# An unread TensorE product ahead of each entry of maxima in the first three steps of a group

## The reference

```
def _L0_attn_ref(x, wq, wk, wv, wo):
    DIM = 512
    N_HEADS = 32
    N_KV_HEADS = 8
...
    hd = D // H
    q = (x @ wq).reshape(B, N, H, hd)
    k = (x @ wk).reshape(B, N, J, hd)
    v = (x @ wv).reshape(B, N, J, hd)
    q = _rope(q, ROPE_THETA)
    k = _rope(k, ROPE_THETA)
...
    scores = jnp.einsum('bhqd,bhkd->bhqk', q, k) / jnp.sqrt(jnp.float32(hd))
    causal = jnp.tril(jnp.ones((N, N), dtype=bool))
    scores = jnp.where(causal[None, None], scores, -jnp.inf)
    weight = jax.nn.softmax(scores, axis=-1)
    out = jnp.einsum('bhqk,bhkd->bhqd', weight, v)
    out = out.transpose(0, 2, 1, 3).reshape(B, N, D)
    return out @ wo
...
    x = L0_attn_x
    xn = _layernorm(x, axis=-1)
    x = x + _L0_attn_ref(xn, L0_attn_wq, L0_attn_wk, L0_attn_wv, L0_attn_wo) + _L0_ffn_ref(xn, L0_ffn_W_up, L0_ffn_W_gate, L0_ffn_W_down)
    xn = _layernorm(x, axis=-1)
    x = x + _L1_attn_ref(xn, L1_attn_Wq, L1_attn_bq, L1_attn_Wk, L1_attn_bk, L1_attn_Wv, L1_attn_bv, L1_attn_Wg, L1_attn_bg) + _L1_ffn_ref(xn, L1_ffn_Wa, L1_ffn_Wp, L1_ffn_w_std, L1_ffn_w_rec)
    return x
```

## Time and profile before

| | us |
|---|---|
| median of 3 runs | 2506.42 |
| the runs | 2490.51, 2506.42, 2521.99 |
| the profiled execution, its own time | 2503.88 |
| its span (first to last instruction) | 2502.1 |
| mean granted TensorE clock in it | 0.974 |

### The profile page before, as it was taken

One profiled execution on the slowest core, in us unless ns is written; L12 is line 12 of the kernel. 1 busy time (PEld: TensorE's weight loads), 2 busy tenths in 40 slices (PEclk: granted clock), 3 DMA queues, 4 the chain that ended last, 5 costly groups with the idle time before them and its releaser, 6 DMA issues. The chain is left out here.

```text
span 2502.1 us, 41728 instructions
## 1 busy us (share of the span) xinstructions
PE 2368.4 (95%) x16236; PEld 1472.2 (59%) x16236; DVE 1743.1 (70%) x2135; ACT 1268.4 (51%) x2432; POOL 510.6 (20%) x444
## 2 busy tenths in 40 slices
PE   8989999999999999999999889989999999999988
PEld 5778877764444444444444557778865555455545
DVE  6664556557888888888683353432279999999986
ACT  4522222227777777877676432222225666556653
POOL 2210000010000000000000002220036766667752
PEclk9999999999999999999799989999999999999999
DMA  6771100014112121120003220007861232220024
GB/s 226 239 190 55 41 27 1 1 21 71 29 36 35 23 54 26 32 41 19 8 22 78 70 85 1 1 0 149 251 143 33 51 70 68 69 52 24 13 80 145
DMA packets 119507, 161.47 MB, mean 65 GB/s; under 512 B 60624, under 2 KB 66288, under 8 KB 113934
## 3 DMA queue, kind: packets, MB, share of 16 engines
q1 hardware_dynamic: 114058, 142.91, 23.1%
q10 hardware_dynamic: 5124, 15.73, 2.0%
q0 software_dynamic: 128, 0.16, 0.0%
HBM read 110.90 MB, written 47.69 MB: 63 GB/s over the span
## 5 line engine op out<-in xcount | busy, mean ns | idle before, releaser
L929 ACT ACTIVATE a_ex<-a_ps_s 128x512 f32<-128x512 f32 (+3 forms) x1280 | 621.4, 533 | 218.4 <-PE a_ps_s L995 141.8
L1085 DVE TENSOR_REDUCE first_space<-a_ps 128x2 f32<-128x1024 f32 (+2 forms) x532 | 541.7, 1047 | 107.6 <-PE a_ps L960 104.7
L1426 ACT ACTIVATE a_ex<-a_ps_s 128x512 f32<-128x512 f32 (+3 forms) x640 | 320.5, 532 | 260.1 <-PE a_ps_s L1520 138.8
L1393 POOL TENSOR_TENSOR a_acc<-a_acc,a_ex 128x512 f32<-128x512 f32 (+3 forms) x288 | 348.9, 1212 | 116.5 <-ACT a_ex L1426 97.9
L1040 PE MATMUL a_ps_o<-a_ex,a_v 128*32 128x256 f32 (+2 forms) x5016 | 359.0, 368 | 8.2 <-ACT a_o L917 7.3
L1596 DVE TENSOR_REDUCE a_mx_part<-a_ps 128x2 f32<-128x1024 f32 (+2 forms) x320 | 336.6, 1055 | 26.3 <-PE a_ps L1472 23.0
L2094 POOL TENSOR_TENSOR gc_z<-gc_state,gc_qg 128x512 f32<-128x512 f32 x16 | 26.3, 1642 | 1078.7 <-DVE gc_qg L2082 1078.7
L1629 DVE TENSOR_TENSOR a_acc<-a_acc,a_ex 128x512 f32<-128x512 f32 (+3 forms) x288 | 243.0, 844 | 2.7 <-ACT a_ex L1426 2.4
L995 PE MATMUL a_ps_s<-a_q,a_k 50*128 50x512 f32 (+2 forms) x720 | 239.9, 414 | 1.9 <-ACT a_ex L929 1.9
L960 PE MATMUL a_ps<-a_k,a_q 48*128 48x512 f32 (+2 forms) x720 | 218.1, 406 | 2.9 <-DVE first_space L1085 2.3
L1040 PEld LDWEIGHTS a_ps_o<-a_ex,a_v 128*32 128x32 f32 x5016 | 104.9, 109 | 166.5 <-ACT a_ex L929 105.6
(11 more groups left out here) (289 smaller groups left out, 4597.2 us busy)
## 6 DMA issues: line engine op xcount, KB each, us to landing
a_q<-q SPq DMA_DIRECT2D x30, 256.0 KB, 4.8
a_k<-k SPq DMA_DIRECT2D x15, 512.0 KB, 4.8
a_q<-q SPq DMA_DIRECT2D x15, 512.0 KB, 6.2
q<-first_k SPq DMA_DIRECT2D x22, 256.0 KB
first_q<-q SPq DMA_DIRECT2D x18, 256.0 KB, 5.1
second_q<-q SPq DMA_DIRECT2D x9, 512.0 KB, 5.5
second_k<-k SPq DMA_DIRECT2D x9, 512.0 KB, 4.6
X<-in_x SPq DMA_DIRECT2D x4, 1024.0 KB, 13.8
```

The source lines that it names most:

```text
L929: act.activation(ex[unit % NE][:, h % 2, off:CH], ps_s[n % 3][:, off:CH], ACT.Exp, scale=SCALE)\
L1085: dve.tensor_reduce(mx_part[:, 2 * p:2 * p + 2, i, kc], bank[:, :, 0:w], AX.X, ALU.max).then_inc(taken1, 1)
L1393: pool.tensor_tensor(total[:, off:CH], total[:, off:CH], tile, ALU.add).then_inc(added0, 1)
L1426: act.activation(ex[s % NE][:, h, off:CH], ps_s[n % 3][:, off:CH], ACT.Exp, scale=SCALE)\
```

## The change

In steps (0,0), (0,1) and (0,2) of every group, each entry of maxima gets one unread product of 512 columns ahead of it. The first six steps of the attention keep their two. `s < FINAL + STEPS` holds for all steps.

```
--- before.py
+++ after.py
@@ -723,6 +723,7 @@
     STEP_LIST = [(g, c, t) for g in range(GROUPS) for c, t in PASS2_STEPS]
     FINAL = len(STEP_LIST) - STEPS
     FILLED = 6
+    SEAM = ((0, 0), (0, 1), (0, 2))
     TAIL = FINAL + 23
     UNIT_AT = {TAIL + 2 * u: u for u in range(2 * KT)}
     SLOTS = {s: range((s + LEAD) * PAIRS, (s + LEAD + 1) * PAIRS) for s in range(len(STEP_LIST))}
@@ -1056,7 +1057,7 @@
                     if n in FLIP_AT:
                         flip(n)
                     if n < len(BLOCKS):
-                        max_scores(n, 2 if s < FILLED else 0)
+                        max_scores(n, 2 if s < FILLED else 1 if (c, t) in SEAM and s < FINAL + STEPS else 0)
                     if p == 1 and (s in UNIT_AT or s - 1 in UNIT_AT):
                         first = s in UNIT_AT
                         if s == TAIL:
```

## The result

The changed kernel takes 2514.46 us in the median of 20 runs (2509.3 to 2556.7); the kernel before, in 20 runs beside it, 2504.88 (2485.83 to 2535.75). The ratio is 1.0069 with a 95% interval from 1.0039 to 1.0099: 0.7% slower, which is no change by a measure of 2%, but a loss beyond its own interval. The profiled execution took 2512.05 us.

What follows compares the result with a forecast made beforehand. The late seam was bound by VectorE, the early seam and rest of the group by TensorE's order; 2503.88 - 15.1 (clock fall removed) + 18.0 (42 products) = 2506.8, predicted as 2507 us, range 2492 to 2524.

Steps and rivals of the forecast that it cites:

- The mechanism: Products fill TensorE's thin stretch in the seam, so the clock stays up; they cost about as much as the fall prevented.
- the signs named: Groups 1 to 7 2.57 us longer (wrong under 1.0 or over 3.5), 66 fill matmuls, no stretch at 0.50 in 552-1345 us.
- part (2) and (3) of the working: Price of one product, 0.33 us plus lost pairing, then summed over the seam's halves: 2.57 us a seam, 18.0 for seven.
- Half by half: Added time in the seam: 0.70 per entry of (0,0), 0.05 and 0.64 in (0,1), 0.48 for (0,2).
- The time from the start of the score product to that of the unread one: Lost pairing in the seam: the 128-row product waits for the score product, 0.43, 0.37 or 0.31 us by columns.
- the entry behind the flip: First entry of step (0,1): its wait for VectorE covers nearly all of the product, leaving +0.05 us.
- The gain of 15.1 us: Group 6's fall in the profiled execution goes: 117.0 us becomes 101.9.
- the level of one fall: Three runs of before, 15.9 and 15.6 us apart, read as none, one and two falls; the median has one.
- Rival (b): Products mostly hidden behind VectorE's backlog in the seam: price 6.7 instead of 18.0 us, total 2495.5; chance 0.17.
- its low bound: Lowest price: no pairing lost and both VectorE waits cover what they can, 0.96 us a seam, 6.7 us in all.
- Rival (a): Clock still falls once a run, in untouched step (0,3) or another thin place: 2521.9 us, 0.6% slower; chance 0.26.
- its rule of idle gaps: Skill page: falls come from TensorE's idle gaps between bursts, so products in the seam's short gaps would cure nothing.

Runs made afterwards that it cites:

- the experiment with two: Changed kernel with two unread products instead of one per entry in the seams of groups 1 to 7: ratio 1.0104 to the kernel before.
- the kernel with the products elsewhere: Changed kernel with the same 42 products moved to steps (1,0), (1,1) and (1,2): median 2538.82 us, ratio 1.0205 to the kernel before.

## Why the prediction held, and where it was off

The forecast was 2507 us in a range of 2492 to 2524, no change by 2%; 2514.46 lies in it. The mechanism was right: the clock fell at a thin place of the seam, the products remove the fall, and they cost as much as it or more. Of the signs named, groups longer by 3.1 us lie under the bound of 3.5, and the fill's line has the 66 products.

The step that was mis-sized is the price, part (2) and (3) of the working: "0.66 for two, 0.33 each". The opening steps show a pair, and half of a pair isn't one: the first costs 0.44, the second 0.23, as the experiment with two shows. Half by half the seam took 0.76, 0.79, 0.17 and 0.73 us more, and the two halves of (0,2) together 0.66, where the working had 0.70, 0.70, 0.05, 0.64 and 0.48. That makes 3.11 instead of 2.57, for seven seams 21.8 instead of 18.0. So 3.8 of the 7.5 us between forecast and median are the price; the profiled execution lies 1.5 over its sum, and the median of all runs 2.2 over that of the lower level (2512.25). The time from the start of the score product to that of the unread one held (0.37 for 384 columns, measured 0.36; 0.31 for 256, measured 0.31 from 773.27 to 773.58), and the entry behind the flip was the cheap one, as said.

The gain of 15.1 us was read for a run with one fall. In the first comparison the runs of before had 0 to 3, and 1.15 on average by their levels; in another series most had none. So the gain isn't a constant of the kernel, and neither is the loss measured. That the median of before lies in the level of one fall, as the forecast took it, was luck of that series.

Rival (b), hidden products, is out: VectorE's waits cover them only if TensorE isn't made late first, as it is in the early seam with 128 rows; with 64 rows it is nearly true (0.68 a seam, below the 0.96 of its low bound). Rival (a), a fall that stays, holds by the granted clock in a third of the runs, though with some 20 us and not 15.1, and no profile shows where. On its rule of idle gaps from the Trainium skill (TensorE: Matmul & The Clock Gate, section "HAM oscillation — how this bites in real kernels"): the trace of the kernel with the products elsewhere shows the clock fall with TensorE busy 2.50 of 3.20 us and no pause over 0.45, so it fell without what the rule asks, and in the kernels with short waits filled or removed the falls in the seam went. What I had not seen is that a delay ahead of the place serves too.

Open: where in the changed kernel the low clock of the upper level lies. Steps (2,9) and (2,10) are a candidate. Open too: why the same seam lets the clock fall in some groups and runs and not in others.

## What to carry to other kernels

Price a filler by what it separates, not by its columns: a product on all rows between two that share the array by rows ended their overlap, and one on the free half of the rows kept the clock in 12 of 12 runs too, at a fifth of the price. Put it only where the clock falls, found by the first low stretch in the table and by what another engine makes TensorE wait for there. Read such a change by the levels and the granted clock of many runs on one chip, since a median may lie on either side of a fall that comes in part of them.

## What the runs showed of the hardware

The clock fell from 1.00 to 0.50 with TensorE busy 2.69 of the 3.40 us ahead of it and no pause between its matmuls over 0.45 us, and the same instructions a group earlier left it up. Once low it stayed so for 37.6 us in before, in which TensorE was busy 37.1 us of 37.4 by the records, and the group took 15.1 us longer; with the products elsewhere it was low from 1099.2 to 1126.5, 27.3 us, with TensorE busy for all of the 27.2 from 1099.3 on, and the group took 11.5 us longer. How many falls a run has differs between series of runs, each on its own chip: before's runs without one were 15 of 23 in one and 6 of 29 in another. A product of 128 rows and 512 columns held the next one back for 0.44 us, two together for 0.67, and one of 64 rows on the free half of the array started together with the score product.
